# First mixer: the keys' decays move from VectorE to GpSimd, and the order of one batch's VectorE work changes

## The reference

```python
xc = _causal_dwconv_silu(x, conv_w)
q, kg, v, g = xc @ wq, xc @ wkg, xc @ wv, xc @ wg + bg
gk = jax.nn.log_sigmoid(kg) / NORMALIZER
k = 1.0 - jnp.exp(gk)
# per head and step: S = S * exp(g_t) + k_t v_t ; o_t = (q_t * scale) S
o = _gla(qh, kh, vh, gkh, scale)
o = o + jax.nn.sigmoid(aug_w[..., None] * vh)
o = (o - mu) * jax.lax.rsqrt(var + LN_EPS)
return jax.nn.silu(g) * o @ wout
...
x = _layernorm(x + _L0_attn_ref(x, ...), axis=-1)
```

## Time and profile before

| | |
|---|---|
| median of 3 runs | 4351.98 us (4350.99 to 4358.85) |
| the profiled execution | 4346.4 us, span 4344.8 us |
| busy in the span | PE 3884.9, DVE 2465.0, ACT 1990.0, POOL 1196.7 us |
| first mixer | about the first 845 us of the span |
| busy tenths there, first 8 of 40 slices | DVE 6 8 8 8 8 8 8 4, POOL 0 1 1 1 1 1 1 1 |

### The profile page before, as it was taken

The page is one execution under the profiler, slowest core; times in us unless marked ns, Lnnn a source line. Parts: engine busy times, 40 slices in busy tenths (PEclk is TensorE's granted clock), DMA queues, the critical chain, the costliest instruction groups (busy, mean ns, idle before and its releaser), DMA issues. The chain is left out here.

```text
span 4344.8 us, 69246 instructions
## 1 busy us (share of the span) xinstructions
PE 3884.9 (89%) x23860; PEld 2993.3 (69%) x23860; DVE 2465.0 (57%) x5456; ACT 1990.0 (46%) x4069; POOL 1196.7 (28%) x1878
## 2 busy tenths in 40 slices
PE   6788888598999999998489999999999999879998
PEld 3555555367888888887267777777777777656665
DVE  6888888462222222221568888888888887421111
ACT  5666666111211212211357777777777777432221
POOL 0111111101122122121345444455455453200000
PEclk8889989699999999999689999999999999889999
DMA  1011001154555555554211111111111111111111
GB/s 36 30 34 41 31 31 33 39 143 161 189 184 181 191 179 183 189 177 162 62 40 40 45 50 45 50 45 45 49 47 45 45 45 27 56 35 53 54 58 48
DMA packets 199445, 347.09 MB, mean 80 GB/s; under 512 B 75396, under 2 KB 150404, under 8 KB 180996
## 3 DMA queue, kind: packets, MB, share of 16 engines
q1 hardware_dynamic: 169284, 271.16, 19.6%
q0 software_dynamic: 29904, 72.65, 5.7%
HBM read 276.61 MB, written 68.16 MB: 79 GB/s over the span
## 5 line engine op out<-in xcount | busy, mean ns | idle before, releaser
L525 ACT ACTIVATE moe_rel<-moe_fc 128x512 f32<-128x512 f32 x284 | 169.5, 597 | 798.4 <-PE moe_fc L490 798.4
L490 PE MATMUL moe_fc<-moe_xT,moe_win 128*128 128x256 f32 x2272 | 503.7, 380 | 1.5 <-issue 0.8
L501 PE MATMUL moe_o<-moe_wout,moe_hT 128*128 128x256 f32 x2272 | 502.0, 379 | 0.0
L490 PEld LDWEIGHTS moe_fc<-moe_xT,moe_win 128*128 128x128 f32 x2272 | 432.7, 191 | 61.1 <-issue 2.1
L501 PEld LDWEIGHTS moe_o<-moe_wout,moe_hT 128*128 128x128 f32 x2272 | 426.4, 190 | 55.0
L549 DVE TENSOR_TENSOR moe_hT<-moe_rel 128x512 f32<-128x512 f32 x284 | 196.6, 692 | 360.7 <-ACT moe_rel L525 360.7
L1743 DVE SCALAR_TENSOR_TENSOR gdr_y<-gdr_bank,gdr_cw,gdr_y 128x511 f32<-128x511 f32 (+2 forms) x384 | 287.3, 748 | 37.3 <-ACT gdr_y L2056 22.9
L558 DVE COPY moe_osb<-moe_o 128x512 f32<-128x512 f32 x71 | 49.1, 691 | 425.0 <-PE moe_o L501 425.0
L2337 PE MATMUL gdr_bank<-gdr_hT,gdr_wqkv 128*128 128x512 f32 x512 | 258.2, 634 | 13.4 <-ACT gdr_qk L2071 7.8
L1305 PE MATMUL gdr_bank<-gdr_hT,gdr_wqkv 128*128 128x512 f32 x512 | 225.3, 599 | 3.5 <-ACT gdr_hT L1323 3.5
L1338 DVE TENSOR_TENSOR gdr_kb<-gdr_bank,gdr_x 128x512 f32<-128x512 f32 x32 | 20.6, 685 | 366.4 <-PE gdr_bank L1314 366.4
(11 more groups left out here) (393 smaller groups left out, 8786.2 us busy)
## 6 DMA issues: line engine op xcount, KB each, us to landing
moe_win<-in_moe_w SPq DMA_DIRECT2D x71, 1024.0 KB, 7.8
moe_wout<-in_moe_w SPq DMA_DIRECT2D x71, 1024.0 KB, 5.2
slots_out<-moe_osb POOLq DMA_DIRECT2D x71, 256.0 KB, 7.5
gdr_fz<-mixed_rows SPq DMA_DIRECT2D x18, 512.0 KB, 3.8
gla_xp<-in_xT_rows SPq DMA_DIRECT2D x16, 512.0 KB, 4.6
gla_xres<-in_x_rows SPq DMA_DIRECT2D x16, 512.0 KB, 3.7
token_rows<-gla_x POOLq DMA_DIRECT2D x16, 512.0 KB, 3.4
rt_W<-in_fc_b SPq DMA_DIRECT2D x32, 256.0 KB, 3.3
```

Source lines behind the costliest of these rows:

```text
L490: ins = nc.tensor.matmul(fc_ps[j][:, m % 2, :], win[u][:, c, m * P:(m + 1) * P], xT[:, c, :], start=(c == 0), stop=(c == DT - 1))
L501: ins = nc.tensor.matmul(o_ps[u][:, t, :], hT[u][:, k, t * P:(t + 1) * P], wout[u][:, k, :], start=(k == 0), stop=(k == FT - 1))
L525: nc.scalar.activation(rel[:, j, :, :], fc_ps[j][:], ACT.Relu).then_inc(relu_done, 1)
```

## The change

Eight differences and eight products of `kt` per batch leave VectorE and stand on GpSimd, whose loop is written out per batch. The head norm's mean and variance of batch b are done at the end of round b instead of in round b+1. The residual sum, its statistics and the closing rows stand ahead of the third output and of both convolutions, and both convolutions ahead of the fourth output. ScalarE's order follows: squares stand behind the SiLU of the convolution, `spread` is split in two halves among the copies of the values. `done("D", ...)` of the decays becomes `Dk`, the scan's event `G`.

```diff
--- before.py
+++ after.py
@@ block.gpsimd
-                with pool.Fori(0, B) as b:
+                pool.wait_ge(set_up, 9)
+
+                def head_rstd(b):
+                    wait, _ = waiter(pool, b)
+                    wait("var", 1)
+                    nc.gpsimd.tensor_tensor(rstd32[:], var32[:], mhalf[:], ALU.pow).then_inc(s["rstd"], 1)
+
+                def differences(b, u):
+                    wait, _ = waiter(pool, b)
+                    wait("G", 1)
+                    if later(b, 1):
+                        pool.wait_ge(s["sc"], (b - 1) * TT)
+                    for a in range(NSUB):
+                        n, r = SUB * (a + 1), SUB * a + SUB // 2 - 1
+                        nc.gpsimd.tensor_tensor(kt[u][:, :, a, 0:n], G[:, :, r:r + 1].broadcast_to([P, NCH, n]), G[:, :, 0:n],
+                                                ALU.subtract).then_inc(s["Dk"], 1)
+
+                def products(b, u):
+                    wait, _ = waiter(pool, b)
+                    wait("k", 1)
+                    for a in range(NSUB):
+                        n = SUB * (a + 1)
+                        wait("E", 5 + a)
+                        nc.gpsimd.tensor_tensor(kt[u][:, :, a, 0:n], kt[u][:, :, a, 0:n], k_[:, :, 0:n], ALU.mult).then_inc(s["kt"], 1)
+
+                def rows_out(b):
...
                     wait("lnvar", 1)
                     nc.gpsimd.tensor_tensor(rstd[:], var[:], mhalf[:, 0:TT], ALU.pow).then_inc(s["lnrstd"], 1)
                     wait("x1", 1)
                     pool.dma_start(dst, x1[:]).then_inc(x1_stored, 16)
                     wait("lg", 1)
                     pool.dma_start(dst2, lg[:]).then_inc(lg_stored, 16)
                     pool.wait_ge(x1_stored, b * 16 + 16)
                     pool.nop().then_inc(x1_free, 1)
...
+                def body(b, u, past, more, far):
+                    w = 1 - u
+                    if past is not None:
+                        head_rstd(past)
+                        if later(past, 0):
+                            logits_kept(past - 1)
+                    if more:
+                        differences(b + 1, w)
+                        products(b + 1, w)
+                    if past is not None:
+                        rows_out(past)
@@ block.vector, gates
-                    Chain(dve, gate_step, b)(v.tensor_tensor_scan(flat(G[:]), flat(notstart[:]), g[:], 0.0, ALU.mult, ALU.add))
+                    if later(b, 0):
+                        dve.wait_ge(s["Dk"], b * NSUB)
+                    done("G", 1, v.tensor_tensor_scan(flat(G[:]), flat(notstart[:]), g[:], 0.0, ALU.mult, ALU.add))
@@ block.scalar, exponents
                         wait("gg", 1)
+                        if later(b, 0):
+                            act.wait_ge(s["kt"], b * NSUB)
                         done("ek", 1, a_op(ab[:], g[:], ACT.Exp))
@@ block.scalar, body
                     if more:
                         gates(b + 1)
-                    if past is not None:
-                        squares(past, w)
-                    if more:
                         exponents(0, b + 1, w)
-                        exponents(1, b + 1, w)
-                        exponents(2, b + 1, w)
                     if past is not None:
                         turned(past, "oTp", "oT", oT)
                     if more:
-                        spread(b + 1, w)
+                        exponents(1, b + 1, w)
+                        exponents(2, b + 1, w)
                         values(0, b + 1, w)
+                        spread(0, b + 1, w)
                         values(1, b + 1, w)
+                        spread(1, b + 1, w)
...
                     if far is not None:
                         silu(b + 2, u)
+                    if inside(b):
+                        squares(b, u)
```

More of the change, by code:

```diff
@@ L737, in _, with logits_kept @@
                     pool.nop().then_inc(x1_free, 1)
+                def logits_kept(b):
                     pool.wait_ge(lg_stored, b * 16 + 16)
                     pool.nop().then_inc(lg_free, 1)
+                def body(b, u, past, more, far):
[9 more added lines that the diff above has]
+                        rows_out(past)
+                starts(body)
+                for b in range(2, B - 2):
+                    body(b, b % 2, b - 1, True, b // 2 + 1)
+                ends(body)
+                logits_kept(B - 1)
             @block.vector
@@ L789, in products @@
-                def products(part, b, u):
-                    wait, done = waiter(dve, b)
-                    if part == 0:
-                        wait("q", 1)
-                        wait("E", 1)
-                        done("qt", 1, tt(qt[:], flat(eR[:]), qs[:], ALU.mult))
-                        wait("E", 2)
-                        done("qhat", 1, tt(qhat[u][:], flat(eG[:]), qs[:], ALU.mult))
-                        wait("k", 1)
-                        wait("E", 3)
-                        done("khat", 1, tt(khat[:], khat[:], k_[:], ALU.mult))
-                        done("aw", 1, tt(aw[:], qs[:], flat(k_[:]), ALU.mult))
-                    else:
-                        for a in range(4 * (part - 1), 4 * part):
-                            n = SUB * (a + 1)
-                            wait("E", 5 + a)
-                            done("kt", a + 1, tt(kt[u][:, :, a, 0:n], kt[u][:, :, a, 0:n], k_[:, :, 0:n], ALU.mult))
+                    ref8 = blocks8(G[:])[:, :, SUB // 2 - 1:SUB // 2].broadcast_to([P, NCH * NSUB, SUB])
@@ new lines, in differences, with products @@
+                    done("D", 1, tt(blocks8(eR[:]), blocks8(G[:]), ref8, ALU.subtract))
+                    done("D", 2, tt(khat[:], G[:, :, CH - 1:CH].broadcast_to([P, NCH, CH]), G[:], ALU.subtract))
+                def products(b, u):
+                    wait, done = waiter(dve, b)
+                    wait("q", 1)
+                    wait("E", 2)
+                    done("qt", 1, tt(qt[:], flat(eR[:]), qs[:], ALU.mult))
+                    done("qhat", 1, tt(qhat[u][:], flat(eG[:]), qs[:], ALU.mult))
+                    wait("k", 1)
+                    wait("E", 3)
+                    done("khat", 1, tt(khat[:], khat[:], k_[:], ALU.mult))
+                    done("aw", 1, tt(aw[:], qs[:], flat(k_[:]), ALU.mult))
@@ L901, in body @@
                     if more:
[L902 removed]
+                        differences(b + 1)
                     if past is not None:
                         tail(0, past)
+                    if recur:
+                        masked(3, b, u)
                     if more:
[L906 removed]
+                        products(b + 1, w)
                     if past is not None:
@@ L909, in body @@
                     if recur:
-                        masked(3, b, u)
                         outputs(2, b, u)
-                    if more:
-                        products(2, b + 1, w)
+                    if past is not None:
+                        tail(2, past)
                     if far is not None:
+                        conv(0, b + 2, u, far)
                         conv(1, b + 2, u, far)
@@ L917, in body @@
                         outputs(3, b, u)
+                        head_norm(0, b, u)
                     if more:
                         own(b + 1, w)
+                    if recur:
+                        head_norm(1, b, u)
+                    if more:
                         masked(0, b + 1, w)
                     if past is not None:
-                        tail(2, past)
+                        tail(3, past)
                 for c in range(DT):
@@ L967, in exponents, with spread @@
                     else:
-                        for a in range(4 * (part - 1), 4 * part):
+                        for a in range(NSUB):
                             n = SUB * (a + 1)
-                            wait("D", 3 + a)
+                            wait("Dk", a + 1)
                             done("E", 5 + a, a_op(kt[u][:, :, a, 0:n], kt[u][:, :, a, 0:n], ACT.Exp))
-                def spread(b, u):
+                def spread(half, b, u):
                     wait, done = waiter(act, b)
                     wait("qt", 1)
-                    for h in range(GH):
+                    for h in range(half * GH // 2, (half + 1) * GH // 2):
                         ins = a_op(qspread[u][:, :, h, :], qt[:].rearrange("p (n i) -> p n i", i=SUB), ACT.Copy, scale=headmask[:, h:h + 1])
-                    done("spread", 1, ins)
+                    done("spread", half + 1, ins)
                 def values(t, b, u):
```

50 lines of the change are left out of this document (13 added, 37 removed).

## The result

The changed kernel takes 4276.68 us in the median (4270.21 to 4278.37, 4 runs) against 4354.03 (4350.99 to 4358.85): a ratio of 0.9816, 95% interval 0.9803 to 0.9829. The prediction said 4275. The profiled execution took 4276.16 us, its span is 4274.2.

The account below looks back on a forecast made before the run. VectorE's own queue was the bound. Per period -7.8 - 3.2 + 4.6 + 0.7 + 0.3 + 0.3 = -5.1 us; 13 periods 66, leading periods 4, end 7: together 77, giving 4275 us, range 4240 to 4316.

Parts of the forecast that it names:

- Three waits: VectorE's waits ahead of the head variance (1.5 us), an output (1.2) and L810 (0.5) all go: 3.2 a period.
- Contention: Nine two-operand VectorE instructions each wait out one GpSimd instruction, 0.51 us each: 4.6 a period; none 0, all 16 8.2.
- (a): New VectorE wait for the closing rstd, between var and the scaling of the closing rows: 0.7 us a period.
- (b): New wait ahead of on: the head's power stands behind the logits' DMA on GpSimd, 0.3 us a period.
- (c): New VectorE wait for TensorE ahead of z: 0 to 1.3 us, taken as 0.3 a period.
- GpSimd: Its 16 kt instructions take 12.7 us, 13.9 with joins, plus 3.1 waiting for VectorE: 17.0; var ends 1.5 later.
- The two leading periods: The two periods ahead of the steady ones, 80.51 us, limited by latencies: gain 0 to 10, taken as 4.
- The end: 16 instructions leave (-7.8 + 4.6) and the 3.92 wait for the second-last head power is covered: gain 7 us.
- no collisions (1): Rival: GpSimd and VectorE hardly collide, 0 instead of 4.6, 60 us more gained: 4215; chance 0.07.
- TensorE (2): Rival: TensorE becomes the bound, its projection at the lower clock adding 2.7 us a period: 4310; chance 0.11.
- GpSimd's queue (3): Rival: GpSimd's kt instructions take twice as long (27 us), delaying closing rows and convolutions: 4430; chance 0.07.
- The power (4): Rival: GpSimd's power also blocks VectorE, at its first S, 4.0 us a period: 4327; chance 0.02.

Follow-up runs that it names:

- before, filled: The kernel before plus constant matmuls, results unread, in TensorE's two idle times of each period: 4362.5 us, ratio 1.0022 to before.
- the idle piece filled: The changed kernel with the 16 kt instructions back on VectorE, plus three constant matmuls in TensorE's idle piece: 4310.9 us, ratio 0.9891 to before.
- the order alone: The changed kernel with GpSimd's 16 kt instructions back on VectorE: 4345.5 us, ratio 0.9982 to before.
- changed, filled: The changed kernel plus two constant matmuls in TensorE's idle time ahead of the projection: 4283.4 us, ratio 0.9838 to before.
- second interleaved order: The changed kernel with VectorE's order rewritten against collisions, aw and closing rows earlier for TensorE: 4254.1 us, ratio 0.9766 to before; with one constant matmul 4241.1.

## Why the prediction was right

The mechanism of the steady periods was right: work leaves VectorE, the order removes its waits, contention takes part of it back. That the time came within 2 us of 4275 is luck: some terms were off by up to 10 us and cancelled.

- **What leaves VectorE**, 7.8: right. Without collisions it is busy 34.85 us for 42.16, 7.3 less, and 16 joins go.
- **Three waits**, 3.2: gone, for the reason given; not TensorE's clock (before, filled). What I missed is that the reordering alone brings another wait, ahead of the masks (1.1 to 6.0 us): it pays only with TensorE's clock mostly at 2.4 GHz, or with the kt products out of the queue ahead of the closing rows. With the idle piece filled, the order is worth 2.2 of the 3.2 a period.
- **Contention**, 4.6: the nine instructions named were caught, and only they; 5.4 in all, 0.60 each, from 0.18 (`D` 1) to 0.95 (`aw`). Bounds 0 and 8.2 held it.
- **(a)** 0.7: measured 0.88. **(b)** and **(c)**, 0.3 each: no wait ahead of `on` or `z`. Instead, in two periods of three, those of 43.4 to 43.6 us, 0.2 to 0.3 each ahead of `kvm`, of the gates (for `l1`) and, but once, of a mask; the periods of 42.9 have none of them.
- **GpSimd**, 12.7 us and 3.1 of waits for VectorE: 14.7 for both. The joins of 0.08 did not show, and 2.0 us of waiting for ScalarE's exponentials, ahead of the products (L743), is missing from the sum; `var` ended 2.7 us after it (predicted 1.5).
- **A period**: -4.4, not -5.1; 13 of them 57 us, not 66.
- **The two leading periods** are the step that failed: 14.0, outside my 0 to 10, of which I took 4. "Limited by latencies" left out whose they are. They were VectorE's waits for TensorE, ahead of `augw` and of an output, of the kind that the order removes in the steady periods. VectorE's waits in the two periods fell from 17.1 to 7.1 us, its busy time from 60.1 to 57.1; the order alone gives 11.6 there. Its longest waits for TensorE before, then after:

```profile
DVE gla_augw L810 <- PE gla_pB L1143: 9.3, 2, 8.8
...
DVE gla_o L837 <- PE gla_pO L1116: 5.3, 1, 5.3
```

```profile
DVE gla_hold L847 <- PE gla_pU L1116: 4.7, 1, 4.7
```

- **The end** gave 9.7 for 7, and not by the term named: the wait of 3.92 is not covered but falls to 2.43, and a wait of 3.07 for logits, which the sum does not have, goes: VectorE's waits there fall from 44.6 to 39.2 us, its busy time from 60.9 to 57.3. So 81 for 77 in all.

```profile
706.64 1.23 DVE L886 TENSOR_TENSOR gla_on<-gla_o,gla_rstd 128x1024 f32<-128x1024 f32 x1 [2.43 <-POOL gla_rstd L725]
```

Of the rivals: no collisions (1) fell with the groups above. TensorE (2) is no bound, but its sign, gates waiting for `l1`, showed: 0.25 us in two periods of three, which are 0.7 us longer than the others (43.62 and 42.90). Ahead of these waits the clock falls to 0.50 for 3.4 us as the projection begins; that the clock makes the whole difference is not shown for this kernel, since filling that idle time moved the fall (changed, filled). In the second interleaved order one filler there took off 1.7 us (41.65 to 39.93). GpSimd's queue (3) had 2.7 us to spare. The power (4) blocks nothing; the timeline has it beside two `S` at their full speed:

```profile
357.27 5.51 POOL L725 TENSOR_TENSOR gla_rstd<-gla_var,gla_mhalf 128x32 f32<-128x32 f32 x1
```

```profile
359.00 1.01 DVE L860 SCALAR_TENSOR_TENSOR gla_S<-gla_S,gla_gE,gla_kvm 128x256 f32<-128x256 f32 x2
```

Here the rule that the loser is blocked for the whole instruction (the Trainium skill, SBUF — State Buffer, Who interferes with whom) does not hold: these two `S`, 0.485 us each before, take 1.01 us together within the power's 5.51.

## What to carry to other kernels

Work that left the busiest engine paid only once the order fed the others: here each half of the change was worth little or less than nothing, and both together 80 us. After such a change, list where TensorE waits and what runs behind the wait: in the order alone an idle piece of 2.9 us ahead of the transposes was followed by 10 to 20 us at 1.2 GHz, in the changed kernel one of 1.7 us ahead of the projection by 3.4. Collisions with GpSimd were ordered away by half at best, from 5.4 us a period to 3.8 and 2.8, since others (the convolution, the closing rows) were caught instead; look first at which of them TensorE waits for.
